# Edges packed without holes, attention in groups of 512 edges, and node scores by two-column fp32 products in a four-layer graph network

## The reference

```python
h = relu(layernorm(x)); x = x + L0(h)   # 3 hyperbolic convolutions: segment_sum(w * ht[src], dst)
h = relu(layernorm(x)); x = x + L1(h)   # attention, edge attributes of width 16, then a layer norm
h = relu(layernorm(x)); x = x + L2(h)   # segment_sum(relu([h[src], h[dst], e8] @ W1 + b1) @ W2 + b2, dst)
h = relu(layernorm(x)); x = x + L3(h)   # attention
```

## Time and profile before

| | us |
|---|---|
| median of 3 runs | 14483.36 (14475.38 to 14483.87) |
| span of the profiled execution | 14473.0 |
| busy: TensorE, weight loads | 9746.3 (67%), 8816.7 (61%) |
| busy: VectorE, ScalarE, POOL | 10317.1 (71%), 5084.8 (35%), 10529.2 (73%) |
| POOL's gathers, 9256 | 9007.0, 973 ns each |

### The profile page before, as it was taken

How to read it: one execution, slowest core, us unless ns; L and a number is a source line. 1 busy time by engine, 2 the same in 40 slices (tenths; PEclk the granted TensorE clock), 3 DMA queues, 4 the chain that set the end, 5 groups by cost and what they waited for, 6 DMA issues and landing times.

```text
span 14473.0 us, 400585 instructions
## 1 busy us (share of the span) xinstructions
PE 9746.3 (67%) x94470; PEld 8816.7 (61%) x94471; DVE 10317.1 (71%) x47961; ACT 5084.8 (35%) x16333; POOL 10529.2 (73%) x10828
## 2 busy tenths in 40 slices
PE   0000006777778888788887788888577777888888
PEld 0000006777767777677777677777455555777777
DVE  7870007777776666666666888888888887888888
ACT  1000000000000000000000788888577676777777
POOL 3777777777767777677777677777577776677776
PEclk9995557888888888888888555555788888555555
DMA  2101112222211111111111111111111111111111
GB/s 101 26 25 26 26 26 47 41 41 41 40 27 27 27 27 27 27 27 27 27 27 25 30 28 27 27 27 27 23 26 26 26 26 24 30 28 28 28 28 30
DMA packets 496417, 441.99 MB, mean 31 GB/s; under 512 B 289869, under 2 KB 315085, under 8 KB 494926
## 3 DMA queue, kind: packets, MB, share of 16 engines
q0 software_dynamic: 346368, 334.42, 13.9%
q1 hardware_dynamic: 149454, 102.38, 2.5%
HBM read 364.93 MB, written 65.20 MB: 30 GB/s over the span
## 4 chain that ended last, share of the span: by engine, by line
PE 39%; issue 18%; DVE 16%; POOL 14%; DVEq 8%; ACT 3%; DMA 2%; ACTq 0%; POOLq 0%; SPq 0%
PE bank L1559 16%; PE bank L1534 11%; POOL packed L450 9%; POOL G L469 4%; DVEq L732 4%; PE bank L1616 3%; PE bank L1628 3%; DMA G<-table,idx 2%; DVE OH L749 2%; PE bank L1605 1%; PE bank L1718 1%; PE bank L1547 1%; DVEq L734 1%; PE bank L1632 1%; DVE OHT L788 1%
## 5 line engine op out<-in xcount | busy, mean ns | idle before, releaser
L469 POOL DMA_INDIRECT G<-table,idx x9256 | 9007.0, 973 | 3237.1 <-issue 2497.9
L1452 ACT ACTIVATE OHB<-bank,const 128x512 bf16<-128x512 f32 x159 | 109.2, 687 | 6718.5 <-PE bank L1547 6718.5
L1559 PE MATMUL bank<-UZ,OHT 128*128 128x192 bf16 x15600 | 2093.5, 261 | 543.5 <-DVE OHT L788 543.5
L1534 PE MATMUL bank<-G,OH 128*128 128x64 f32 x9984 | 1683.9, 300 | 589.0 <-DVE OH L749 449.6
L450 POOL DMA_INDIRECT packed<-Y,slab_pos x1568 | 1522.0, 971 | 671.5 <-issue 495.4
L1559 PE MATMUL bank<-UZ,V 128*128 128x192 bf16 x14976 | 1994.0, 259 | 0.0
L1534 PEld LDWEIGHTS bank<-G,OH 128*128 128x128 f32 x9984 | 1494.1, 217 | 760.2 <-DVE OH L749 678.6
L1559 PEld LDWEIGHTS bank<-UZ,OHT 128*128 128x128 bf16 x15600 | 1511.1, 111 | 583.0 <-DVE OHT L788 561.4
L1534 PE MATMUL bank<-ZR,OH 128*128 128x65 f32 x6656 | 1765.4, 419 | 1.8 <-DVE ZR L887 1.8
L1534 PEld LDWEIGHTS bank<-ZR,OH 128*128 128x128 f32 x6656 | 1623.8, 334 | 2.1 <-DVE ZR L887 2.0
L749 DVE TENSOR_SCALAR OH<-const,DL,W 128x128 f32<-128x128 f32 x4992 | 1560.6, 367 | 0.2 <-issue 0.2
(11 more groups left out here) (303 smaller groups left out, 21034.3 us busy)
## 6 DMA issues: line engine op xcount, KB each, us to landing
G<-table,idx POOLq DMA_INDIRECT x9256, 2.5
packed<-Y SPq DMA_DIRECT2D x42, 640.0 KB, 17.7
UZ<-packed SPq DMA_DIRECT2D x104, 256.0 KB, 2.7
Y<-in_payload SPq DMA_DIRECT2D x98, 256.0 KB
packed<-Y,slab_pos POOLq DMA_INDIRECT x1568
table<-Y SPq DMA_DIRECT2D x6, 1690.0 KB, 5.5
idx<-SRC SPq DMA_DIRECT2D x624, 8.0 KB
X<-in_x SPq DMA_DIRECT2D x1, 1568.0 KB, 8.0
```

Of the source, the lines that this page charges most:

```text
L469: pool.indirect_dma_start(out=G[:, 2 * q + c, :], out_offset=None, in_=table, in_offset=bass.IndirectOffsetOnAxis(ap=idx[:, h, j:j + 1], a ...
L1534: o = pe.matmul(ps_a[r % 2][:, 0:w], OH[:, q, c, :], parts[c], start=c == 0, stop=c == 1)
L1559: o = pe.matmul(ps_rows[c // 2][:, c % 2 * 3 * D:(c % 2 + 1) * 3 * D], tile_hot(tile)[:, c * P:(c + 1) * P], table_parts[:, tile, :, :].re ...
```

## The change

Edges are packed without holes: position = rank of the edge among all edges. 200704 slots are NGR = 784 groups of 256, or NGA = 392 groups of 512. Consumers walk items, pairs of (group, tile that has an edge in it): NG = 832 items of 256 in message and MLP passes, NA = 440 items of 512 edges in attention. Edges of the group outside the tile have a local target outside 0 to 127, so that no one-hot holds them; in attention MASK lowers their own score. A word per item (`item_words`) holds tile and group. The registers of an iteration give tile (`Tiles`, a shift) and place (`Slots`, the word & 63) of the rows; G becomes a ring of RING = 4 chunks of 16 groups (8 in attention), and POOL gathers NCH = 49 chunks instead of 52 iterations. SP counts landed groups in `rows_here`, for which VectorE (messages, attention) or ScalarE (MLP) waits once every four items (`need_rows`). The columns from the on-chip table are made in iterations 0 to 48; iterations 49 to 51 have none.

The fill of the packed area is gone and its pitch is 2048 slots instead of 1680. Loading moves from SP to ScalarE's queue: in pass 0 (`first_pass`), per iteration, 16 fetches of a group, two stores of the 8 attributes to HBM by item (`store_e8`) and 16 copies of two source indices per partition from item order to group order (`to_groups`); in pass 1 (`second_pass`) 8 fetches of 512 edges per iteration, which VectorE unpacks (`unpack_a`). The MLP pass loads its attributes once an iteration from ScalarE's queue. AHEAD is 5 instead of 3.

In attention the one-hots, V, its transposes and the maximum are 512 edges wide, in rings of 4 and 2 items. OHT is fp32 (ring of 2), node score and shift lie beside each other in `pair`, and `to_edges` is one fp32 product of two columns per 128 edges. The bf16 splitting of score and shift is gone.

The diff, cut to its core:

```diff
-NG = -(-((N_EDGES + T * (GE - 1)) // GE) // BODY) * BODY
+CA = 4
+BODY_A = 8
+NGR = KC // 2
+NCH = NGR // BODY
...
-NS = 1680
...
+NGA = KC // CA
+NA = -(-(-(-N_EDGES // (CA * P)) + T - 1) // BODY_A) * BODY_A
+ITER_A = NA // BODY_A
+RING_A = 8
+PEELED_A = 9
+RING = 4
+COLS = RING * 2 * BODY
 ITER = NG // BODY
...
+        def steps(eng, body, lag, on_chip=False):
             for u in range(BODY):
-                body(u, 0)
-            with nc.Fori(1, ITER, engines=[eng.engine], hint_back_edge=True) as i:
+                body(u, 0, on_chip)
+            if on_chip:
+                with nc.Fori(1, NCH, engines=[eng.engine], hint_back_edge=True) as i:
+                    body(None, i, True)
+            with nc.Fori(NCH if on_chip else 1, ITER, engines=[eng.engine], hint_back_edge=True) as i:
+                body(None, i, False)
+            for u in range(lag):
+                body(u, ITER, False)
+        WORD_OF, FIRST_OF = range(2)
...
+        def need_rows(eng, n, quad, u, i):
+            if u % 4 == 2 or (u == 0 and isinstance(i, int)):
+                eng.wait_ge(rows_here, (quad[(u + 2) // 4 if u else 0] & 1023) + (ROWS_BEFORE[n] + 1))
         def ds(start, size):
...
+                def rows_of(i, last):
+                    for h in range(2):
+                        end = min(BODY // 2 * (h + 1), fetched(n))
+                        for q in range(BODY // 2 * h, end):
+                            sp.wait_ge(gathered[LANDS[n]][q], i * 32 + (landed(n) + 32))
+                            if PLAN[n][0] != ATT or q % 2 == 1:
+                                sp.sem_inc(rows_here, 1)
+                        if not last:
+                            indices(i + 1, h)
+                    for q in range(fetched(n), BODY):
+                        if PLAN[n][0] == GCN:
+                            sp.wait_ge(taken[q - fetched(n)], i + (n * NCH + 1))
+                        else:
+                            sp.wait_ge(taken_e, i + 1)
+                        sp.sem_inc(rows_here, 1)
...
+                def gathers(i, slot):
...
+                            if kind != ATT:
+                                need(pool, used, i * (BODY * each) + ((before_n + q - BODY + 1) * each - late))
+                            elif q % 2 == 0:
+                                need(pool, used, i * BODY_A + (before_n + q // 2 - 2 * BODY_A + 1))
...
+            def item_words(ks, cum_of, bits, top, to):
+                n_j = ks.shape[-1]
+                by_tile = [P, n_j, T]
+                before = before_flat[:, 0:n_j * T].rearrange("p (j t) -> p j t", t=T)
+                f0, f1 = sched_f[:, 0, 0:n_j], sched_f[:, 1, 0:n_j]
+                tt(before, cum_of[:, 0:T].unsqueeze(1).to_broadcast(by_tile), ks.unsqueeze(2).to_broadcast(by_tile), ALU.is_le)
+                reduce64(f0, before)
+                tt(before, before, extra[:, 0:T].unsqueeze(1).to_broadcast(by_tile), ALU.mult)
+                reduce64(f1, before)
+                tt(f1, ks, f1, ALU.subtract)
+                ts(f1, f1, float(top), None, ALU.min)
+                own.wait()
+                own.count(v.scalar_tensor_tensor(to, f0, float(1 << bits), f1, ALU.mult, ALU.add))
...
+                def weighted_one_hot(g, u, i, q, quad):
                     need(v, agg_ready, g + (gb - 7))
+                    need_rows(v, n, quad, u, i)
                     for c in range(2):
                         at = bass.ds(g * 2 + c, 1)
...
+                def own_scores(g, u, r, words):
+                    need(v, v_ready, g * 2 + (2 * kb - 14))
+                    if u % 4 == 0:
+                        v.wait_ge(rows_here, (words[u + 3 + LAG] & 511) + (ROWS_BEFORE[n] + 1))
+                    scores = GA_groups[:, bass.ds(words[u + LAG] & 63, 1), :, D].rearrange("p a s -> p (a s)")
+                    v.tensor_tensor(EL[:, r, :], scores, own_score[:, ds(g * CA, CA)], ALU.add).then_inc(el_ready, 1)
+                def one_hot(g, u, q):
+                    need(v, oht_ready, g + (eb - 3))
+                    v.tensor_tensor(OHB_A[:, q, :, :], iota_b[:, :].unsqueeze(1).to_broadcast([P, CA, P]),
+                                    DLw[:, CA * u:CA * u + CA].unsqueeze(2).to_broadcast([P, CA, P]),
+                                    ALU.not_equal).then_inc(oh_ready, 1)
+                def largest(g, r):
+                    v.wait_ge(x_ready, g + (kb + 1))
+                    need(v, dm_done, g + (kb - 7))
+                    v.tensor_reduce(sr["gm"][:, r:r + 1], ps_x[r % 2][:, :], AX.X, ALU.max).then_inc(a_done, 1)
...
+                def node_score(g, r, t):
+                    need(v, of_edge, g + (kb - 7))
+                    move(pair[:, r, 0:1], small["er"][:, bass.ds(t, 1)]).then_inc(b_done, 1)
...
+                def shift(g, r, u):
+                    last, first = pair[:, (r - 1) % 8, 1:2], RESw[:, u + LAG:u + LAG + 1]
+                    v.wait_ge(a_done, g * 3 + (3 * kb + 3))
+                    need(v, shift_ready, g + kb)
+                    need(v, dm_done, g + (kb - 6))
+                    v.scalar_tensor_tensor(pair[:, r, 1:2], last, first, sr["a2"][:, r:r + 1],
+                                           ALU.max, ALU.min).then_inc(shift_ready, 1)
...
+                def step(u, i, words):
...
+                    g = i * BODY_A + u
+                    edges = exponents(g - 3, (u - 3) % 8) if live(3) else iter(())
+                    if live(4):
+                        weigh(g - 4, (u - 4) % 8, words[u - 4 + LAG] & 63)
+                    if live(2):
+                        largest(g - 2, (u - 2) % 8)
+                        node_score(g - 2, (u - 2) % 8, words[u - 2 + LAG] >> 9)
+                    if live(0):
+                        own_scores(g, u, u % 8, words)
+                    next(edges, None)
+                    if live(2):
+                        bound(g - 2, (u - 2) % 8)
+                    next(edges, None)
+                    if live(2):
+                        sloped_bound(g - 2, (u - 2) % 8)
+                    if live(0):
+                        one_hot(g, u, u % 4)
+                    next(edges, None)
+                    if live(2):
+                        shift(g - 2, (u - 2) % 8, u - 2)
+                    if live(5):
+                        add_up(g - 5, (u - 5) % 8, words[u - 5 + LAG] >> 9)
...
+            def unpack_a(j):
...
+                    own.count(move(DLA[:, at], buf[:, :, DST_AT].bitcast(I32)))
+                    tt(prod16[:, :, :], buf[:, :, E16_AT:E16_AT + D16],
+                       ve[:, :].unsqueeze(1).to_broadcast([P, PIECE, D16]), ALU.mult)
+                    local = DLA[:, at].rearrange("p (g s) -> p g s", s=CA)
+                    own.count(v.scalar_tensor_tensor(local, tile_of, -float(P), local, ALU.mult, ALU.add))
+                    reduce64(EAV[:, at], prod16[:, :, :])
+                    own.count(v.tensor_scalar(MASK[:, at], DLA[:, at], 0.0, None, ALU.is_lt))
+                    stt(MASK[:, at], DLA[:, at], float(P - 1), MASK[:, at], ALU.is_gt, ALU.add)
+                    ts(MASK[:, at], MASK[:, at], NO_SCORE, None, ALU.mult)
+                    own.wait()
+                    v.tensor_tensor(EAV[:, at], EAV[:, at], MASK[:, at], ALU.add).then_inc(unpacked, 1)
...
+                        if c % 2 == 1:
+                            o.then_inc(v_ready, 1)
+                    need(a, agg_ready, g + (gb - 3))
+                    a.activation(OH_A[:, q, :, :], OHB_A[:, q, :, :], ACT.Identity, scale=-1.0, bias=ones[:, 0:1])
+                    a.wait_ge(mt_ready, g + (eb + 1))
+                    need(a, of_edge, g + (kb - 1))
+                    a.activation(OHT_A[:, r % 2, :, :], ps_m[r % 2][:, :].rearrange("p (s c) -> p s c", s=CA),
+                                 ACT.Identity, scale=-1.0, bias=ones[:, 0:1]).then_inc(oht_ready, 1)
...
+                def store_e8(j):
+                    for h in range(2):
+                        a.wait_ge(pack_in[h], j * (16 * half) + 16 * half)
+                        at = ds((j * 2 + h) * (half * 2 * D8), half * 2 * D8)
+                        a.dma_start(e8_items[:, at].rearrange("p (s c) -> p s c", c=D8),
+                                    pack_buf[h][:, :, E8_AT:E8_AT + D8]).then_inc(e8_out[h], 16)
+                def to_groups(i):
+                    first = items_of(a, FIRST_OF, i, 0, 2 * NG - 2)
+                    need(a, src_in, i * (16 * BODY))
+                    for q in range(BODY):
+                        a.dma_start(SRC[:, ds(i * (2 * BODY) + 2 * q, 2)],
+                                    SRCI[:, bass.ds(first[q], 2)]).then_inc(src_in, 16)
...
+                def each(i, fetching):
+                    a.wait_ge(unpacked, (i + AHEAD) * 2 + 3)
+                    if fetching:
+                        fetch(i + AHEAD + 1)
+                    to_groups(i + 2)
+                    code_made(0, i + 1)
+                    if fetching:
+                        store_e8(i + AHEAD + 1)
```

(27 more changed lines are left out.)

879 lines of the change are left out of this document (502 added, 377 removed).

## The result

| | us |
|---|---|
| kernel before, 4 runs beside it | 14479.37 |
| changed kernel, 4 runs | 13989.42 (13984.28 to 13993.57) |
| ratio | 0.9663, 95% interval 0.9649 to 0.9676 |
| span of the profiled execution | 13988.5 (before: 14473.0) |

A forecast was written before the change was run, and what follows sets the result against it. POOL's queue was taken as the bound everywhere. Setup +10, start of pass 0 +60, passes 0 to 2 -265, MLP -100, attention +75, splitting -5 sum to -225 us: 14258, said as 14255, range 13900 to 14560.

The forecast's parts named there:

- POOL's rate and 8722 gathers: All passes over the edges: a gather costs POOL 1.25 to 1.28 us, and packing leaves 8722 gathers, 534 fewer.
- Start of pass 0: Between last scatter and first gather: loads on ScalarE's queue delay the first gather, +60 us (bounds +20 and +120).
- 3.7 us an iteration in which TensorE goes idle: Pass 1: VectorE's attention unpacking adds this to each iteration, so the pass gains only 60 us.
- it fits narrowly into 52 iterations: MLP pass: VectorE's work fits 52 iterations at 37 us, so the pass gains 100 us (bounds 0 and -118).
- Setup: Before the first position: VectorE computes two more schedules, and POOL's scatters move with them, +10 us.
- The item is 4.87 us ... and TensorE passes POOL: Both attention passes: TensorE needs 4.87 us per 512-edge item against POOL's 4.53, +75 us (bounds -5 and +313).
- POOL's queue is the bound everywhere: Kernel before, all stages: gathers and scatters at 1.28 us take 13.8 of 14.47 ms.
- Rival 1: Attention stays bound by POOL through cheap two-column products or a rising TensorE clock: 13960 us, chance 0.15.
- its second: Attention: the other reason for POOL staying the bound, that TensorE's clock rises from the granted 0.50; no separate size.
- The rule of the Trainium skill: Attention: loads at columns/1.2 ns and a 25 ns floor make a two-column product 0.27 us, both passes POOL-bound.
- Rival 2: Attention becomes a chain with exposed hand-overs: no faster from 5.13 us per item, 14900 us at 5.6; chance 0.14.
- rivals 3 and 4: ScalarE's queue bounds pass 0, 14580 us, chance 0.06; packing gives message and MLP passes nothing, 14620 in full, chance 0.10.

The follow-up runs named there:

- e9: Changed kernel with the one-hot in four instructions and first source indices moved to group order after two loaded chunks instead of four: 13904.97 us, ratio 0.9604.
- e16: Changed kernel with the one-hot in four instructions, first source indices after two chunks, and ScalarE's first code before the second set of indices: 13901.77 us, ratio 0.9605.
- e8: Changed kernel with one group of 256 edges in four not gathered in the last attention pass: 13950.23 us, ratio 0.9638 to the kernel before.
- e7: Changed kernel with each two-column fp32 product of to_edges issued twice into the same place: 15403.31 us, ratio 1.0639 to the kernel before.
- e5: Changed kernel with VectorE's attention one-hot written by four instructions of 128 columns instead of one of 512: 13914.14 us, ratio 0.9618 to the kernel before.
- e6: Kernel before with the gathers of one group in sixteen left out: 13999.56 us, ratio 0.9672 to the kernel before.
- e14: Kernel before with one group in sixteen not gathered and VectorE's attention one-hot made for one column of two: 13962.15 us, ratio 0.9648.
- e3: Changed kernel with each two-column product of to_edges issued twice, on a slower chip: ratio 1.0259 to the kernel before there.
- e12: Kernel of e16 on a slower chip: ratio 0.9900 to the kernel before there.

## Why the forecast was too small

- **POOL's rate and 8722 gathers:** right. "POOL: 49 x 35.8 = 1754" is 1760 from first to last gather in passes 0 and 2.
- **Start of pass 0:** right, 57 of 60 us. The price of a chunk on ScalarE's queue (12 to 15 us) is 13.7, although a fetch moves 32 KB and not the 64 KB of the forecast. e9 and e16 add that undoing it isn't worth its full length.
- **Pass 1, "3.7 us an iteration in which TensorE goes idle":** VectorE is busy 1401.16 us against 1216.37 in pass 2, 3.8 us an iteration, so the work was priced rightly, but both passes last 1770 us. The unpacking is covered; 30 us too little was forecast.
- **MLP, "it fits narrowly into 52 iterations":** it fits, -124 against -100 (bound -118). **Setup:** +23 instead of +10. Neither was taken further.
- **Attention, "The item is 4.87 us ... and TensorE passes POOL":** this is the step that failed. The item is 4.50 us (trace, e8). The price of one two-column fp32 product was sound (e7: 0.43 us); the sum of the parts was not. Each part was too long by its starts in the new item: bf16 transposes by 0.06 us, fp32 transposes by 0.05, sums by 0.09, products by 0.16. They had been priced in a group of half the width, with a hand-over of its own, or from products that stood alone. Together with the rounding that is 0.37 us too much for each of 440 items, 163 us a pass. Corrected for that alone the stage is 1980 + 17 = 1997 us. It takes 2043 and 2041, and POOL does pass TensorE by a little, for a reason that wasn't in the forecast at all: POOL's gathers grow from 958 to 996 ns under VectorE's wide one-hot. With that taken away (e5) the two passes, from first gather to last sum, fall from 2068 and 2048 us to 2019 and 2019.
- **"POOL's queue is the bound everywhere":** wrong for attention, and by chance without harm to the sum. e6 shows that the old step had its own 41.2 us an iteration. Packing alone, with groups of 256 edges, was not run; by e6 it would have left these passes nearly where they were, so the item of 512 edges must be what lets them follow. VectorE's timeline of the changed kernel shows how. Its shift (L1157) in four items in a row, with the window move of an iteration between the first two:

```profile
9033.08 0.21 DVE L1157 SCALAR_TENSOR_TENSOR pair<-pair,RESw,r_a 128x1 f32<-128x1 f32 x1
9033.85 0.17 DVE L624 TENSOR_SCALAR RESw<-RES 128x16 f32 x1
...
9038.73 0.21 DVE L1157 SCALAR_TENSOR_TENSOR pair<-pair,RESw,r_a 128x1 f32<-128x1 f32 x1
...
9042.22 0.21 DVE L1157 SCALAR_TENSOR_TENSOR pair<-pair,RESw,r_a 128x1 f32<-128x1 f32 x1
...
9046.61 0.21 DVE L1157 SCALAR_TENSOR_TENSOR pair<-pair,RESw,r_a 128x1 f32<-128x1 f32 x1
...
9069.91 0.17 DVE L624 TENSOR_SCALAR RESw<-RES 128x16 f32 x1
```

The step with the register load is 5.65 us, the next 3.49, then 4.39: most of the head of an iteration is made up for at once. The same 4096 edges take 36.06 us (9033.85 to 9069.91) instead of 41.2; the mean of the pass is 8 x 4.61 = 36.9. VectorE is busy 1242 us of 2043 and not 1762.61 of 2135, which would explain it, but no run shows that this is the cause: e14, with less work for VectorE in the old step, won back only 0.45 us an iteration.

- **The rivals.** Rival 1 (attention stays bound by POOL, 13960) came within 30 us, and its sign came too: POOL waits in attention for almost nothing, where the forecast wanted it to wait for VectorE's weighting. Its first reason, "the two-column products are cheap", holds only in so far as the whole item was; its second fails, for the clock stayed at 0.50, also where TensorE was busy 1000.00 of 1000 us (e8). The rule of the Trainium skill ("TensorE: Matmul & The Clock Gate", LDWEIGHTS and Back-to-back issue gap) that made the item 4.2 us is not borne out: a product costs 0.43 us in e7, where an estimate by that page had 0.27. Rival 2 (a chain, 5.13 us or more) didn't come: the item of 4.50 us has no gap. Of rivals 3 and 4 nothing showed.
- **The range.** The forecast's "own range from its bounds", 14130 to 14480, is narrower than its bounds added up (14064 to 14921), and it doesn't say how they were combined. That the time, 13989, lies inside the wider range is owed to the weight given to rival 1.

## What to carry to other kernels

Price a pipelined item from starts in a stretch that has the new form of back-to-back work, or take the sum over one whole period; parts priced one by one were each a little too long, and here that turned a gain of an attention pass into a forecast loss. Before a stage is called bound by one engine because its rate fits, take work from that engine and see whether the stage follows: two paces can agree by chance (40.9 and 41.2 us here). Look at what a wide instruction does to another engine's short ones, not only at its own time: 0.2 us more on VectorE's idle side bought 75 us (e5). And see whether the step with periodic extra work (register loads, window moves) is made up for within the period: 4.4 us weren't in the old step, most of 1.2 us were in the new one.

## What the runs showed of the hardware

A gather issued by POOL that begins while VectorE writes a wide bf16 one-hot (128 x 512, 0.69 us) ends late, as if held until shortly before that instruction ends. In pass 3 of the changed kernel those that began 0.04 to 0.07 us into it took 0.49 to 0.51 us more, those 0.1 to 0.2 us into it 0.42 us, those 0.3 to 0.4 us into it 0.19 us. One that begins together with it is not held: in pass 5, 58 gathers began in the first 0.04 us of a one-hot, and none took over 0.01 us more. So the length of a pass hangs on how the two engines fall into step: the mean gather is 995 ns in pass 3 and 982 in pass 5, where it was 959 and 960. VectorE's weighting (fp32, 128 x 256, 0.42 us) holds gathers too, by 0.21 us at most; its maximum, which reads PSUM, holds none. Nor is the effect new: in the kernel before the one-hot of 256 columns (0.42 us) held gathers by up to 0.25 us. Four narrow instructions in place of the wide one still cost a gather 0.08 us at their start, but bring the mean in the stretch back to 960 ns (e5), 75 us in all. The Trainium skill ("SBUF — State Buffer", SBUF: two separate sides) has a reason for it: a DMA issued from POOL's queue has its descriptors written by POOL, which is shut out of the port it shares with VectorE while VectorE runs in a mode that uses both. The runs agree in the effect and about in its length; that the port is the cause no run here shows apart.

Among other products, each further two-column fp32 product of 128 weight columns costs 0.43 us at clock 0.50 (1.2 GHz; e7), as much as one of 65 columns (four sums in 1.71 us). So with so few columns the moving columns don't set the price. That the weight loads do is a reading, not shown apart: they are busy 1957.47 us beside TensorE's 1972.74 in pass 3.

Three of the six chips of the experiments ran every kernel about 37% slower at nearly the instruction durations of the others (gather median 947 ns in e3, 944 in the changed kernel); the time lies between instructions. On one of these e16's kernel (there e12) had a ratio of 0.9900 to the kernel before instead of 0.9605. A gain of this kind is therefore one of the chip too, and the cause of those gaps is open.
